# A hybrid block on one core: the delta rule's 32-row system solved by blocks, with right side and inverse in one operand, and work handed to ScalarE

## What is computed

```python
q, k, v = silu(conv4(x @ W...)); q = l2norm(q) * 128**-0.5; k = l2norm(k)
g = exp(-softplus(x @ Wfa @ Wfb + dt_bias) * exp(A_log)); beta = sigmoid(x @ Wb)
def step(S, (qt, kt, vt, gt, bt)):       # per batch, head and token
    S = S * gt[..., None]
    delta = (vt - einsum('bhk,bhkv->bhv', kt, S)) * bt[..., None]
    S = S + kt[..., None] * delta[:, :, None, :]
    return S, einsum('bhk,bhkv->bhv', qt, S)
o = o * rsqrt(mean(o*o) + 1e-6) * norm_w * sigmoid(x @ Wga @ Wgb);  return o @ Wo
```

## Time and profile before

| what | value |
|---|---|
| median of 3 executions | 2618.57 us |
| the profiled execution | 2619.83 us |
| its span | 2618.0 us |
| TensorE matmul busy (PE) | 2441.7 us, 93% |
| VectorE (DVE) | 2122.1 us, 81% |
| ScalarE (ACT) | 1408.8 us, 54% |
| GpSimd (POOL) | 1273.1 us, 49% |
| granted TensorE clock, mean | 0.983 |

### The profile page before, as it was taken

The page is one execution under the profiler, slowest core; times in us unless marked ns, Lnnn a source line. Parts: engine busy times, 40 slices in busy tenths (PEclk is TensorE's granted clock), DMA queues, the critical chain, the costliest instruction groups (busy, mean ns, idle before and its releaser), DMA issues.

```text
span 2618.0 us, 102732 instructions
## 1 busy us (share of the span) xinstructions
PE 2441.7 (93%) x46512; PEld 1462.9 (56%) x46512; DVE 2122.1 (81%) x3249; ACT 1408.8 (54%) x2647; POOL 1273.1 (49%) x989
## 2 busy tenths in 40 slices
PE   6799999999999999999999999989899898998989
PEld 3466666666666666666666666664333333333333
DVE  3778888888989888989899888863349999999981
ACT  3555555555655565566566655542465646455332
POOL 0556555555555555655555555540035645545530
PEclk8899999999999999999999999999999999999999
DMA  1000000000000000000000000010023323333320
GB/s 55 23 10 14 14 23 14 13 14 14 24 14 14 14 24 14 14 14 24 13 14 17 21 14 14 7 58 1 26 74 99 130 92 126 106 105 121 129 85 16
DMA packets 52069, 105.61 MB, mean 40 GB/s; under 512 B 7084, under 2 KB 11948, under 8 KB 51376
## 3 DMA queue, kind: packets, MB, share of 16 engines
q1 hardware_dynamic: 51632, 99.04, 11.5%
HBM read 96.65 MB, written 2.37 MB: 38 GB/s over the span
## 4 chain that ended last, share of the span: by engine, by line
PE 77%; DVE 11%; issue 6%; ACT 4%; POOL 1%; DMA 0%; SPq 0%; DVEq 0%; ACTq 0%
PE bank L381 13%; PE bank L483 7%; DVE hs L1705 6%; PE bank L446 5%; PE bank L631 4%; PE bank L1522 4%; PE pair L599 4%; PE pair L589 3%; PE bank L571 3%; PE bank L605 2%; PE bank L544 2%; PE bank L553 2%; PE bank L415 2%; PE pair L1444 2%; PE bank L594 2%
## 5 line engine op out<-in xcount | busy, mean ns | idle before, releaser
L673 DVE SCALAR_TENSOR_TENSOR cv<-raw,taps,cv 128x1024 f32<-128x1024 f32 x288 | 407.0, 1422 | 16.0 <-ACT cv L939 14.7
L2011 POOL TENSOR_TENSOR dBu<-dtu,Bn 128x1024 f32<-128x1024 f32 x128 | 306.1, 2393 | 229.5 <-DVE hc L1712 224.6
L381 PE MATMUL bank<-xn,W 128*128 128x512 f32 x768 | 378.3, 616 | 0.0
L938 ACT ACTIVATE raw<-bank 128x512 f32<-128x512 f32 x192 | 114.7, 598 | 401.3 <-PE bank L381 400.3
L1522 PE MATMUL bank<-hc,eye 128*128 128x512 f32 x512 | 255.1, 627 | 56.7 <-DVE hc L1712 56.6
L1909 ACT ACTIVATE bank<-dtv,m_A 128x512 f32<-128x512 f32 x256 | 174.4, 687 | 210.1 <-DVE hs L1705 209.4
L1198 POOL TENSOR_TENSOR kL<-kL,tot 128x512 f32<-128x512 f32 x128 | 199.8, 1561 | 163.3 <-PE bank L446 162.2
L381 PEld LDWEIGHTS bank<-xn,W 128*128 128x128 f32 x768 | 137.4, 192 | 135.1 <-issue 131.2
L1522 PEld LDWEIGHTS bank<-hc,eye 128*128 128x128 f32 x512 | 93.9, 195 | 206.6 <-DVE hc L1712 116.8
L1712 DVE TENSOR_TENSOR hc<-hs,Cn 128x1024 f32<-128x1024 f32 x128 | 172.8, 1350 | 7.9 <-PE bank L1522 3.7
L1200 POOL TENSOR_TENSOR R<-R,tot 128x512 f32<-128x512 f32 x128 | 165.3, 1291 | 0.0
(11 more groups left out here) (267 smaller groups left out, 5579.2 us busy)
## 6 DMA issues: line engine op xcount, KB each, us to landing
Bn<-ssm_rows SPq DMA_DIRECT2D x128, 256.0 KB, 3.5
Cn<-ssm_rows SPq DMA_DIRECT2D x128, 256.0 KB, 3.2
W<-in_head_w SPq DMA_DIRECT2D x32, 448.0 KB, 3.4
WO<-in_out_w SPq DMA_DIRECT2D x32, 192.0 KB, 2.4
xT<-in_xT SPq DMA_DIRECT2D x1, 2048.0 KB, 8.0
out_xT<-xT SPq DMA_DIRECT2D x4, 512.0 KB, 3.7
xn<-in_w_gate SPq DMA_DIRECT2D x1, 1024.0 KB, 6.5
xn<-in_w_up SPq DMA_DIRECT2D x1, 1024.0 KB, 8.3
```

The costliest lines, as they stand in the source:

```text
L381: m = pe.matmul(psum[bank][:, :], w[:, (kind * KT + k) * P:(kind * KT + k + 1) * P], xn[:, k, b, cols], start=k == 0, stop=k == KT - 1)
L673: dve.scalar_tensor_tensor(cv[m % 2][:, :, :], raw[m % 2][:, :, i:i + SEG], taps[:, h, KQV[n], i:i + 1], cv[m % 2][:, :, :], MUL, ADD).the ...
L2011: pool.tensor_tensor(dBu[at % AHEAD][:, :, :], dtu[s][:, half * DT2:(half + 1) * DT2, :], spread(Bn[at % DEEP][:, :], 1, DT2), MUL).then_i ...
```

## The change

TensorE:

- `dots` multiplies k with [k | q] in one operand (kq, 64 columns) and q with q. The first product of `products`, k against the q of the same token, is gone with it (L454).
- `inverse` starts after the fifth level, with N (a unit diagonal, preset once, and the k parts of all levels). It carries U, the block-diagonal part already inverted, and M, the right side, side by side in `UM`. Four blocks multiply `Et` with [U | M]: the first has 32 columns, the next two have 64, and the last of the four also has 64. A fifth block of 32 columns gives the inverse.

VectorE:

- There is one predicated copy a level, of both parts (512 elements), into `DG`. `Bc`, `bm`, `side`, `Ac` and `on_diag` are gone.
- Beta is applied once, to the finished inverse, so `kT` and `AT` are plain copies.
- Each inverse step is one masked product from PSUM and one transpose.

ScalarE:

- Softplus becomes Abs, Relu, Exp(-|z|) and Ln(1 + .), and VectorE's minimum is gone.
- ScalarE takes over the copies to `AT`, `Bo`, `Y64` and `kT`, and the scaling of the output by its rstd (8 instructions of 128 columns in place of one on VectorE).

GpSimd:

- `bm`, `side`, `AT` and `Y64` are gone, and two products of 256 elements (`bsI`) come in.

Five presets on VectorE (`Y64`, `AT`, `DG`) and two predicated copies stand at the start. The numbers of PLACES, EARLY_AT and FRONT_AT are new, and FFN_AT is not.

```diff
 PLACES = [
-    (-1, [61.85, 106.12, 122.1, 139.6, 143.3, 146.82]),
+    (-1, [62.44, 98.25, 98.25, 107.3, 135.23, 144.87]),
...
@@ -390,16 +391,22 @@ att_tensor
-                        o = psum[bank][quad(w4), (j * NC + c) * SUBB:(j * NC + c + 1) * SUBB]
-                        m = pe.matmul(o, block(t, c, w4 // 2, w4 % 2), block(t, c, w4 // 2, w4 % 2))
+                            if j == 0:
+                                o = psum[bank][quad(w4), c * CH:(c + 1) * CH].rearrange("p (a i) -> p a i", a=2)
+                                m = pe.matmul(o, block(t, c, b, u), kq[s][:, :, c, b, u * SUBB:(u + 1) * SUBB])
...
-                            m = pe.matmul(psum[PROD][quad(2 * b + u), c * SUBB:(c + 1) * SUBB], block(kL[s], c, b, u),
-                                          block(qn[s], c, b, u))
...
-                for li in range(1, NL):
-                    pe.wait_ge(*x_set.at(g, li - 1))
-                    blocks(Bc[li % 2][:, :, :], X).then_inc(z_made.sem)
...
-                    pe.wait_ge(*z_kept.at(g, li - 1))
-                    blocks(Y, Z[:, :, :]).then_inc(dx_full.sem)
+                for li in range(NL - 1):
+                    pe.wait_ge(*et_set.at(g, li))
+                    if li == 0:
...
+                        blocks(lambda q, c: inv[q, 1, c, :], Et, lambda q, c: UM[q, 1, c, :])
+                    else:
+                        pe.wait_ge(*um_set.at(g, li - 1))
+                        blocks(lambda q, c: inv[q, :, c, :], Et, lambda q, c: UM[q, :, c, :])
...
+                blocks(lambda q, c: inv[q, 0, c, :], UM[:, 0, :, :], lambda q, c: Et[q, c, :])
@@ -647,6 +659,15 @@ att_vector
+            dve.memset(Y64[:, :, :, :], 0.0)
+            for i in range(2):
+                dve.memset(AT[i][:, :, :], 0.0)
+                dve.memset(DG[i][:, N_PART, :, :], 0.0).then_inc(blocks_preset.sem)
...
-                    dve.copy_predicated(Ac[:, :, :], mask(1 + li).bitcast(I32), view[:, :, 1, :]).then_inc(diag_set.sem)
-                    dve.tensor_tensor(Bc[li % 2][:, :, :], view[:, :, 0, :], bm[:, li, :, :], MUL).then_inc(level.sem)
+                    dve.copy_predicated(DG[s][:, N_PART:A_PART + 1, :, :], spread(mask(1 + li), 1, 2).bitcast(I32),
+                                        view.rearrange("p c a i -> p a c i")).then_inc(na_set.sem)
...
+                dve.tensor_tensor(UM[:, 1, :, :], DG[s][:, N_PART, :, :], bsI[:, :, :], MUL).then_inc(e0_set.sem)
+                dve.tensor_tensor(UM[:, 0, :, :], UM[:, 1, :, :], mask(1 + NL), MUL).then_inc(e0_set.sem)
+                dve.transpose(et, u).then_inc(et_set.sem)
...
+                    dve.tensor_tensor(E[:, :, :], inv[:, 1, :, :], mask(2 + NL + li), MUL).then_inc(e_set.sem)
+                    dve.transpose(et, e).then_inc(et_set.sem)
...
+                dve.tensor_tensor(XY[:, 0, :, :], inv[:, 0, :, :], spread(bs[s][:, :], 2, SUBB), MUL).then_inc(x_set.sem)
+                dve.transpose(y, x).then_inc(y_set.sem)
...
-                dve.tensor_tensor(og[:, :, :], og[:, :, :], spread(rstd_o[:, :], 2, P), MUL).then_inc(og_scaled.sem)
@@ -985,12 +1006,16 @@ att_scalar
+                    act.activation(soft_z[:, :, :].rearrange("p b n -> p (b n)").rearrange("p (c b t) -> p b c t", b=NB, t=CH)[:, b, :, :],
+                                   psum[bank][:, :].rearrange("p (c t) -> p c t", t=CH), ACT.Abs, bias=dt_bias[:, h:h + 1])
...
-                                   ACT.Identity, bias=dt_bias[:, h:h + 1]).then_inc(gz_set.sem)
+                                   ACT.Relu, bias=dt_bias[:, h:h + 1]).then_inc(gz_set.sem)
...
+                for w in range(4):
+                    u = w % 2
+                    m = act.activation(AT[s][quad(w), :, u * SUBB:(u + 1) * SUBB], DG[s][quad(w), A_PART, :, :], ACT.Copy)
...
+                    act.activation(UM[:, lo:hi, :, :], inv[:, lo:hi, :, :], ACT.Copy).then_inc(um_set.sem)
...
+                for w in range(4):
+                    m = act.activation(Y64[quad(w), :, w % 2, :], XY[quad(w), 1, :, :], ACT.Copy)
...
+                    act.activation(kT[g % 2][:, 4 * q:4 * q + 4, :].rearrange("p c d -> p (c d)"), psum[bank][:, :],
+                                   ACT.Copy).then_inc(kT_set.sem)
...
+                for c in range(NC):
+                    m = act.activation(og[:, c, :], og[:, c, :], ACT.Copy, scale=rstd_o[:, c:c + 1])
```

More of the change, by code:

```diff
@@ L815, in turn_k @@
                     yield
[L816 to L822 removed]
+                turn.next()
+                yield
+                turn.next()
             def solved(g):
@@ L1039, in turn_k @@
                     yield
-                turn.next()
-                yield
-                turn.next()
+                for q in range(2):
+                    bank = turn.next()
+                    act.wait_ge(*k_turned.at(g, q))
+                    if q == 0 and g >= 2:
+                        act.wait_ge(*outer_full.at(g - 2, NC - 1))
+                    act.activation(kT[g % 2][:, 4 * q:4 * q + 4, :].rearrange("p c d -> p (c d)"), psum[bank][:, :],
+                                   ACT.Copy).then_inc(kT_set.sem)
+                    if q == 0:
+                        yield
             def solved(g):
@@ L1153, in dots @@
             def dots(g):
-                for _ in range(3):
+                for _ in range(4):
                     yield
@@ L2142 @@
     masks = [j == col] + [(j // (2 * h) == col // (2 * h)) & (j // h % 2 == 0) & (col // h % 2 == 1) for h in LEVELS]
-    masks += [0 * col + np.broadcast_to((np.arange(P)[:, None] // SUBB) % 2 == u, (P, SUBB)) for u in range(2)]
+    unit, upper = masks[0].astype(np.float32), [m.astype(np.float32) for m in masks[1:]]
+    masks += [unit - m for m in upper] + [1.0 - unit]
     arrays = {
```

336 lines of the change are left out of this document (175 added, 161 removed), and 24 rows, old and new, of the table FRONT_AT.

## The result

The changed kernel takes **2580.65 us** (median of 4 runs, 2575.39 to 2584.55) against 2618.28 on the same chip for the kernel before: a ratio of 0.9849, 95% interval 0.9836 to 0.9862. The forecast was 2590, range 2558 to 2626. The profiled execution has a span of 2576.3 us against 2618.0, 41.7 less.

The account below looks back on a forecast made before the run. The prediction took TensorE's queue to bound the attention phase. Its terms, -40 - 5 + 10 + 1.6 + 1.5 + 4 = -28, against the profiled 2619.8 gave 2592; with the median 1.3 lower, 2590 us, range 2558 to 2626.

Parts of the forecast that it names:

- TensorE's own work: Inverse blocks, dots and first product on TensorE: 1.26 us less a unit, -40 us over 32 units.
- B: Rival: 64-column blocks in 32x32 tiles cost double, 1.36 us; 2622 us, no change; chance 0.07.
- C: Rival: width is free, 64-column blocks cost what 32 columns cost, 0.68 us in the inverse; 2544 us; chance 0.05.
- Waits that go: TensorE's idle time before the inverse's blocks and L454, mostly for issue, partly vanishes: -5 us, bounds -11 and 0.
- Waits that come: The inverse's chain, with work queued ahead on VectorE, makes TensorE 0.3 us late a unit: +10 us, bounds 0 and +16.
- VectorE: VectorE gets 4 us less work a unit, from 46 to 42 of 51, counted as slack: 0.
- ScalarE: ScalarE gets about 11 us more a unit, to 82%; TensorE's work covers the scalings' 2.6 us: 0.
- rival A: ScalarE holds TensorE, its scalings and copies delaying the W copy and bank releases: slower, 2645 us; chance 0.14.
- Start: Presets before the first centring +1.6 us, and unfilled inverse gaps in the first unit +1.5 us.
- Last units: In the last unit the FFN's matmuls no longer fill gaps between state-chain steps: +4 us, bounds 0 and +12.
- Tail: The part after the attention phase has the same instructions in a slightly other order: 0, bounds +-5 us.

Follow-up runs that it names:

- experiment 2: Changed kernel with the k part of the dots as two matmuls of 32 columns in place of one of 64: 2643.6 us, ratio 1.007.
- experiment 11: Changed kernel with each of the inverse's three 64-column steps as two runs of 64 matmuls of 32 columns: 2758.8 us, ratio 1.0521.
- experiment 10: Kernel before, with the DMA of the next W held back until TensorE finished the W products two units earlier: 2604.5 us, ratio 0.9945.
- experiment 5: Changed kernel with GpSimd's two small products (bsI) moved a product level later, behind level 1's: 2565.0 us, ratio 0.9772.
- experiment 4: Changed kernel with the output scaling put back on VectorE as one instruction, off ScalarE's eight: 2658.9 us, ratio 1.013.
- experiment 3: Changed kernel with eight more small ScalarE instructions, into a spare buffer, just ahead of the eight scalings: 2589.3 us, ratio 0.9864.
- experiment 9: Kernel before, with the output scaling as eight ScalarE instructions in place of VectorE's one: 2662.6 us, ratio 1.0159.
- experiment 7: Changed kernel with the early FFN block spread over the last unit's inverse and state steps again: 2578.3 us, ratio 0.9822.

## Why the prediction was right

It was right in sign and nearly in size (2590 for 2581), and by its own steps partly for reasons that don't hold. It took 35 us off the units (-40 - 5 + 10) and put 7 on the ends; measured are 56 off the pitches and 14 on the ends. That both terms were too small and against each other is luck. So is the make-up of the first: the steady unit fell by 0.80 us, where the forecast says about 0.95 (1.26 less 0.3), and the disturbed units, which it had only in its -5, gave some 34 us. Of its signs, L474 came every 50.0 to 51.0 us in those 27 pitches and not 51.2 to 51.7, VectorE is at 86% and not 82%, and the first centring starts at 14.74 (14.3).

**TensorE's own work, forecast -40, measured -51.4** in busy time. The prices are right: 0.68 and 1.03 us for the inverse's blocks (rows above), 4.45 us a unit, as worked out. The two blocks of the dots mostly take 1.03 and 0.69, 0.07 more than the forecast for the second. Rivals B (1.36) and C (0.68) fall by these rows. The rest of the 51 comes from blocks that took longer before than their first row: over six late units L483 took 5.53 us (5.44 forecast), and L381, whose instructions are the same, 11.28 against 10.99 now. By the Trainium skill's rule ("TensorEngine Tiling (Array Packing)", section "Instruction Overhead": a matmul of free dimension 1 has the latency of one of 60) the second 32 of 64 columns would be nearly free. The trace has 1.03 us against 0.68.

**Waits that go, forecast -5, bounds -11 and 0.** Too small: between 200 and 1600 us 10.8 + 2.7 us of waits for issue went, and over the whole span L483 had 18.7 of idle time, where L486 has 3.8. I had put them down by share of blocks and said that they might move on. They are best read as holes in TensorE's supply of instructions (the last section), and with over a sixth of its instructions gone, nearly all went. Experiments 2 and 11 bring them back by adding instructions, experiment 10 thins them out by moving a load, and with them go 20 of the 40 us by which the units of the kernel before stood above 51.04. The other half has no experiment.

**Waits that come, forecast +10, bounds 0 and +16.** Too small as well: L609 waits 23.8 us between 200 and 1600 and 28.3 in all. The forecast named the right kind (the subtraction behind taps in VectorE's queue), at 0.3 us a unit in place of 0.8, and in the inverse's chain. It is at the unit's first outer product, and the two products that GpSimd was given, priced at 0, are one of its causes: 1.68 and 1.58 us for 256 elements, while VectorE's L775 beside them takes 1.21 and not 0.69 (experiment 5). The errors of these two terms are against each other.

**VectorE, forecast 0.** The step that failed. Its slack was reckoned by the unit's mean (42 of 51 us), but for 15.5 us of each unit the chain runs through it and ScalarE, and there it has none. Its share of the page's chain went from 11% to 23%. The scaling that left it costs 78 us where it is put back: 1.5 us a unit of wait, 46 us, and the rest by the slower clock that comes with it (experiment 4). The forecast's rule was that a microsecond off VectorE alone is worth only slack. It fits the late units of the kernel before, where TensorE was idle 0.1 us, and the change itself broke it; no run moved VectorE's work alone there.

**ScalarE, forecast 0; rival A.** Right for the changed kernel (no long row waits for ScalarE, the scalings took 2.44 us where 2.6 was set; experiment 3), and the reason given, that TensorE's own work covers them until it needs W, holds with little to spare: with eight instructions more ahead of the W copies, TensorE waits 0.9 us a unit for them. The scalings also stand behind the copy of Y, which the forecast did not mention; experiment 9 shows A happening where they stand ahead of it. A was the right thing to fear and 0.14 not too much.

**Start, forecast +3.1, measured -2.4** (by L528; -6.7 by L474). The presets cost about what they should; the first unit's line is earlier all the same, which I had not expected. **Last units, forecast +4, bounds 0 and +12: measured +18.7** by L528, out of its bounds. Less dependent on the line is the sum of both ends, +16.3 or +13.8 where +7 was forecast. The mechanism (missing filler) gives 2.7 us in experiment 7. **Tail, forecast 0: right.**

**What the parts are worth.** Taken out of the changed kernel one at a time, three of its parts cost 63, 178 and 78 us (experiments 2, 11, 4), while the whole gained 38, and one of them put alone into the kernel before cost 44. Such numbers don't add: each undoing also breaks the order that was written for the rest, and each makes TensorE wait so much that its clock drops as well (33 of the 78 us in experiment 4).

## What to carry to other kernels

Where one engine is at 98% and another at 86%, both may bound the kernel, in turns within one pass: read the chain of waits over a pass, not the busy shares, before pricing work on the second engine at nothing. An in-order queue is tuned by its order: one conv tap moved behind one subtraction gave 18 us, as much as half of the whole change. Count instructions and not only their time where matmuls are small: a wide one for two narrow ones buys freedom from holes that no row of its own duration shows. And before a loss is put down to a chain of waits, compare the granted clock of the units: part of it may be the same work at 1.2 GHz.

## What was not expected of the hardware

- TensorE seems to run dry of instructions within dense runs of small matmuls. The instruction queue moved 5.98 MB in 365 packets before and 4.95 MB in 302 now, 16,384 bytes each. The 16,384 TensorE instructions (matmuls and weight loads) that went took 63 packets with them, the 4,096 that experiment 2 adds bring 16 more and the 12,288 of experiment 11 bring 48, so a packet holds about 256. A run of 128 32-column matmuls with their loads uses that many in 1.4 us, while a packet's own time is 0.9 to 1.4 us. Of the holes over 0.9 us within a block, between 140 and 1700 us, there are 9 in the kernel before, 15 in experiment 2, 37 in 11 and 3 in 10; **every one of these 64 ends 1.2 to 1.6 us after an instruction packet is in**, however long it is, and begins 0.0 to 1.5 us after that packet's start. The packets come 4.3 to 4.9 us apart in the median, so chance would put about one hole in ten there (an estimate: 0.4 us of each interval). That TensorE waits there for its instructions rests on this and on experiments 2, 10 and 11.
- Idle time of TensorE can be paid a second time in clock. Between 150 and 1700 us the granted clock falls to 1.2 GHz 35 times in the kernel before and experiments 2 and 11, and 31 of these falls come within 6 us behind a hole. In experiment 4, with no hole but 2.3 us of waits a unit in place of 0.8, it falls 16 times, 82 us in all. In the changed kernel and in experiment 10 it doesn't fall there at all. Not every wait brings it: over its pitches experiment 9 has 36 us more idle time than the kernel before and only 7 us more at 1.2 GHz.
- GpSimd and VectorE slow each other. The same GpSimd product of 256 elements takes 0.61 us and 1.68, and VectorE's L782 0.69, 1.21 or 2.00 us. This goes with what GpSimd runs beside it: 1.21 in the first half, with bsI's second product and then R's beside it, and 1.99 in the second half, 1.4 of it beside R's. Being beside is not enough: in the first unit L782 takes 0.69 with 0.6 us of bsI's product beside it. What decides was not tested.
